# f16 projections in the first attention, and the second attention's maxima, value products, closing steps and roots rearranged

## The reference

```python
# L0 attention: 16 heads of 64, causal
q, k, v = x @ Q_w + Q_b, x @ K_w + K_b, x @ V_w + V_b        # per head
scores = softmax(where(causal, -1e5, q @ k.T / 8))
out = sum_h((scores @ v) @ O_w[h]) + O_b
# L0 feed-forward, 512 wide
h = silu(x @ w1.T * s1) * (x @ w2.T * s2)
h = gelu(h @ h1.T * t1); h = gelu(h @ h2.T * t2); out = h @ w3.T * s3
# L1 attention: 16 heads of 8, not causal, with a Gaussian bias G on the scores
G[q, j] = -2 (j - P[q])**2 / Z[q]**2          # P, Z from tanh and sigmoid of the queries
out = softmax(q @ k.T / sqrt(8) + G) @ v @ wo + bo
# L1 feed-forward
out = x @ (W + up_aux @ lora_up @ lora_down @ down_aux).T + b
```

## Time and profile before

| | |
|---|---|
| median of 3 runs | 1842.44 us (1840.41 to 1842.91) |
| the profiled execution | 1839.43 us, its span 1837.7 us |
| mean granted TensorE clock | 0.962 |
| busy PE, DVE, ACT, POOL | 1607.1, 1268.6, 963.1, 644.1 us |
| first attention | 0 to about 820 us |
| feed-forward and second projections | to about 1053 us |
| second attention | from 1053 us; its turns from 1102 us |

### The profile page before, as it was taken

One profiled execution on the slowest core, in us unless ns is written; L12 is line 12 of the kernel. 1 busy time (PEld: TensorE's weight loads), 2 busy tenths in 40 slices (PEclk: granted clock), 3 DMA queues, 4 the chain that ended last, 5 costly groups with the idle time before them and its releaser, 6 DMA issues. The chain is left out here.

```text
span 1837.7 us, 27256 instructions
## 1 busy us (share of the span) xinstructions
PE 1607.1 (87%) x10432; PEld 497.5 (27%) x10432; DVE 1268.6 (69%) x2301; ACT 963.1 (52%) x1109; POOL 644.1 (35%) x363
## 2 busy tenths in 40 slices
PE   7899999999999999987999468888888888888885
PEld 3233333333333333223444211111111111111122
DVE  5767575766666666613332498888888888888866
ACT  3444444444444444432343306777777777777773
POOL 1587877878788878890000100000000000000000
PEclk8999999999999999997999658999999999999997
DMA  5000000000000000001013420111211211111000
GB/s 133 12 8 12 14 12 13 13 7 13 12 12 14 7 18 7 19 7 32 2 48 71 121 39 9 29 28 29 38 23 23 40 23 23 23 23 23 1 2 23
DMA packets 76212, 46.36 MB, mean 25 GB/s; under 512 B 22159, under 2 KB 74931, under 8 KB 76083
## 3 DMA queue, kind: packets, MB, share of 16 engines
q1 hardware_dynamic: 75266, 44.43, 11.5%
q10 hardware_dynamic: 816, 0.20, 0.0%
HBM read 25.66 MB, written 9.31 MB: 19 GB/s over the span
## 5 line engine op out<-in xcount | busy, mean ns | idle before, releaser
L1465 ACT ACTIVATE probs<-ps_e 128x1024 f32<-128x1024 f32 x512 | 500.1, 1021 | 234.8 <-PE ps_e L1539 233.7
L304 POOL TENSOR_TENSOR acc<-acc,probs 128x1024 f32<-128x1024 f32 (+3 forms) x256 | 502.9, 1964 | 86.5 <-ACT probs L338 65.6
L338 ACT ACTIVATE probs<-ps_e 128x1024 f32<-128x1024 f32 (+1 forms) x320 | 285.7, 901 | 377.5 <-PE ps_e L474 128.6
L1648 DVE TENSOR_REDUCE maxpart<-ps_x 128x2 f32<-128x1024 f32 x351 | 427.8, 1219 | 55.0 <-PE ps_x L1503 52.2
L1549 PE MATMUL ps_o<-probs,v 128*9 128x512 f32 x2048 | 268.7, 597 | 45.4 <-ACT probs L1465 30.0
L491 PE MATMUL ps_o<-probs,v 128*64 128x512 f32 (+3 forms) x1280 | 305.6, 556 | 0.2 <-ACT pv_raw L345 0.2
L582 DVE TENSOR_REDUCE maxpart<-ps_x 128x2 f32<-128x1024 f32 x192 | 234.5, 1221 | 75.7 <-PE ps_x L406 75.7
L1455 POOL TENSOR_TENSOR yt<-x_sb,end_b 128x512 f32<-128x512 f32 x4 | 5.1, 1271 | 749.8 <-DVE x_sb L1709 749.8
L1652 DVE TENSOR_REDUCE maxpart<-ps_y 128x1 f32<-128x512 f32 x322 | 220.2, 684 | 19.0 <-PE ps_y L1503 16.0
L1539 PE MATMUL ps_e<-qrows,krows 62*128 62x512 bf16 x1024 | 221.2, 383 | 6.1 <-DMA qrows<-maxrow 5.5
L1503 PE MATMUL ps_x<-krows,qrows 60*128 60x512 bf16 x702 | 152.7, 402 | 69.4 <-DVE maxpart L1648 68.8
(11 more groups left out here) (247 smaller groups left out, 1460.4 us busy)
## 6 DMA issues: line engine op xcount, KB each, us to landing
qrows<-q_rows SPq DMA_DIRECT2D x64, 192.0 KB
rbc<-rden SPq DMA_DIRECT2D x128, 64.0 KB, 2.1
q_rows<-parts_q SPq DMA_DIRECT2D x24, 128.0 KB, 2.4
k_rows<-parts_k SPq DMA_DIRECT2D x24, 128.0 KB, 2.4
krows<-k_rows SPq DMA_DIRECT2D x16, 192.0 KB, 5.9
raw_h<-in_L_ffn_h_w SPq DMA_DIRECT2D x2, 1024.0 KB, 6.6
w_rows<-parts_w SPq DMA_DIRECT2D x6, 256.0 KB, 2.6
qrows<-a_rows SPq DMA_DIRECT2D x64, 24.0 KB
```

The lines of the kernel that those rows point to most:

```text
L304: pool.tensor_tensor(acc[:, u % 2, :, o:], acc[:, u % 2, :, o:], probs[:, turn % RING, :, o:], ALU.add)\
L338: act.activation(probs[:, turn % RING, :, o:], ps_e[:, turn % 2, :, o:], ACT.Exp, scale=1.0 / math.sqrt(D0))\
L1465: act.activation(probs[:, HG * (turn % 2) + hh], ps_e[:, e % 2], ACT.Exp).then_inc(s_ex, 1)
L1648: dve.reduce_max(maxpart[:, at:at + op[2]], ps_x[:, 0:op[2], :], AX.X).then_inc(s_xf, 1)
```

## The change

In the first attention: the projections of pairs 1 to 7 are three f16 products (high by high, high by low of x, low of the weights by high) in place of one f32 product. The high and low parts of x (written over x_sb) and of the weights (from a staging area in raw["h1"]) are made by POOL ahead of its accumulations. The load of h1 is issued by ACT at turn 8. `out_bias` stands ahead of the eighth maxima block instead of behind turn 1's scores.

In the second attention: ps_x and ps_y become three single banks ps_r, used in turn, each with its own pair of semaphores; every maxima block is a product and a reduction of its own. In a turn the eight blocks go two to a head, "fin" behind the second of them, and "mt" behind all eight. In a unit's second turn the value products are at hh 1 and 3 (`late`). The closing steps have new slots; the first two "ct" stand ahead of the last unit. The roots come from POOL (a power, and for all but the last quarter a Newton round), with statistics and normalization apart on DVE; in the last quarter DVE does one Newton round.

```diff
@@ first attention: loads, splits, projections @@
-            for n, dst in (("k", wk), ("q", wq), ("v", wv)):
-                sp.dma_start(dst[:, 2:, :], a[f"L0_attn_{n.upper()}_w"].rearrange("h m d -> m h d")[:, 2:, :]).then_inc(s_ldw[n], 16)
+            for n in "kq":
+                sp.dma_start(w_stage[n].rearrange("p (h d) -> p h d", d=D0),
+                             a[f"L0_attn_{n.upper()}_w"].rearrange("h m d -> m h d")[:, 2:, :]).then_inc(s_wst, 16)
...
+            for g in range(4):
+                pool.wait_ge(s_xtc[g], 1)
+                if g == 0:
+                    pool.wait_ge(s_xt, 4)
+                pool.tensor_copy(x_part[:, g, 0, :], xt[:, g * QC:(g + 1) * QC]).then_inc(s_hx, 1)
+                pool.wait_ge(s_hx, g + 1)
+                pool.tensor_tensor(x_part[:, g, 1, :], xt[:, g * QC:(g + 1) * QC], x_part[:, g, 0, :], ALU.subtract).then_inc(s_xs, 1)
+            pool.wait_ge(s_wst, 32)
+            for i, n in enumerate("kq"):
...
+                pool.tensor_copy(hi_w, w_stage[n]).then_inc(s_hw, 1)
+                pool.wait_ge(s_hw, i + 1)
+                pool.tensor_tensor(lo_w, w_stage[n], hi_w, ALU.subtract).then_inc(s_ws, 1)
...
+                if turn == 8:
+                    act.wait_ge(s_ws, 2)
+                    act.dma_start(raw["h1"][:, :, :], a["L0_ffn_h1_w"].rearrange("(t p) i -> p t i", p=P)).then_inc(s_ldf, 16)
...
-                w = (wk if n == "k" else wq)[:, 2 * p:2 * p + 2, :].rearrange("m h d -> m (h d)")
-                return pe.matmul(out, w, xt[:, c * QC:(c + 1) * QC], start=True, stop=True)
...
+                for m, (w_at, x_at) in enumerate(((0, 0), (0, 1), (1, 0))):
+                    w = w_part[n][w_at][:, 2 * p - 2:2 * p, :].rearrange("m h d -> m (h d)")
+                    mm = pe.matmul(out, w, x_part[:, c, x_at, :], start=m == 0, stop=m == 2)
+                return mm
...
             for g in range(1, 4):
                 first_values(g)
                 max_products(3 + g)
+            out_bias()
             for b in range(7, EARLY):
                 max_products(b)
...
-                elif turn == 1:
-                    out_bias()
@@ second attention: banks and plan @@
-        ps_x = psum("ps_x1", [P, 2, QC])
-        ps_y = psum("ps_y1", [P, QC])
+        ps_r = psum("ps_r1", [P, 3, QC])
...
+            def place(op, bank=None):
+                k = last.index(min(last)) if bank is None else bank
...
+                bank = 2 if turn >= (NU - 1) * TU - 1 else None
+                if turn < 0:
+                    turns.append([place(op) for op in ops[:BU + 1]] + [place(op) for op in extra] + [place(op) for op in ops[BU + 1:]])
+                else:
+                    turns.append([place(op) for op in ops[:2]] + [place(op, bank) for op in extra if op[0] == "fin"]
+                                 + [place(op) for op in ops[2:]] + [place(op, bank) for op in extra if op[0] == "mt"])
@@ PE's turn loop @@
             for turn, ops in enumerate(TURNS):
-                rest = list(ops)
+                rest, late = list(ops), turn % TU == 1
                 for hh in range(HG):
                     scores(turn, hh)
                     for op in rest[:1]:
                         ring(op)
-                    rest = rest[1:]
-                    if hh % 2 == 0 and turn > 0:
+                    if hh % 2 == late and turn > 0:
                         pv(turn - 1, hh // 2)
-                        if len(rest) > HG - 1 - hh:
-                            ring(rest[0])
-                            rest = rest[1:]
+                    for op in rest[1:2]:
+                        ring(op)
+                    rest = rest[2:]
                     if turn >= (NU - 1) * TU and (turn % TU, hh) in PE_SLOT:
                         step(*PE_SLOT[turn % TU, hh])
                 for op in rest:
                     ring(op)
+                if turn == (NU - 1) * TU - 1:
+                    step("ct", 0)
+                    step("ct", 1)
@@ closing steps and roots @@
+        PE_SLOT = {(0, 1): ("wo", 0), (0, 3): ("wo", 1), (2, 1): ("xt", 0), (2, 3): ("xt", 1), (3, 1): ("ct", 2),
+                   (3, 3): ("ff", 0), (4, 1): ("wo", 2), (4, 3): ("ff", 1), (6, 1): ("xt", 2), (7, 1): ("ff", 2)}
...
+                root = pool.tensor_tensor(rstd[:, m], veps[:, m], power[:, :], ALU.pow)
+                if c < NQ - 1:
+                    chained(root)
+                    chained(pool.tensor_tensor(newton[:, :], rstd[:, m], rstd[:, m], ALU.mult))
+                    chained(pool.tensor_tensor(newton[:, :], newton[:, :], veps[:, m], ALU.mult))
+                    chained(pool.tensor_scalar(newton[:, :], newton[:, :], -0.5, 1.5, ALU.mult, ALU.add))
+                    root = pool.tensor_tensor(rstd[:, m], rstd[:, m], newton[:, :], ALU.mult)
...
-                link(dve.tensor_scalar(t1[:, :].bitcast(I32), veps[:, :].bitcast(I32), 1, None, ALU.arith_shift_right))
-                link(dve.tensor_scalar(rstd[:, :].bitcast(I32), t1[:, :].bitcast(I32), -1.0, float(ROOT_SEED), ALU.mult, ALU.add))
-                for _ in range(3):
...
             def refine(kind, c):
+                link(dve.scalar_tensor_tensor(t1[:, m], veps[:, m], -0.5, rstd[:, m], ALU.mult, ALU.mult))
+                link(dve.tensor_tensor(t1[:, m], t1[:, m], rstd[:, m], ALU.mult))
+                link(dve.scalar_tensor_tensor(rstd[:, m], t1[:, m], 1.5, rstd[:, m], ALU.add, ALU.mult))
```

More of the change, by code:

```diff
@@ L512, in first_values, with out_bias @@
                 values(ps_e[:, g // 2, g % 2], 0, g).then_inc(s_pj, 1)
+            def out_bias():
+                pe.wait_ge(s_ldw["o"], 48)
+                pe.wait_ge(s_xtc[3], 1)
+                for p in range(NPAIR):
+                    mm = pe.matmul(ps_o[:, 0:1], wo[:, p, :], bv[:, p:p + 1], start=p == 0, stop=p == NPAIR - 1)
+                mm.then_inc(s_ob, 1)
             x_features(0)
@@ L538, in _ @@
             pe.wait_ge(s_pjv, 4)
[L539 to L544, removed]
             for turn, (xs, ys) in enumerate(PLAN):
@@ L1396, in build, with blocks_of @@
[L1396 to L1399, removed]
-        X_OPS = sum(op[0] == "x" for ops in PLAN for op in ops)
-        Y_OF["fin", NU - 1] = Y_LAST
-        X_DONE, Y_DONE = {}, {}
-        for ops in PLAN:
-            for op in ops:
-                if op[0] in ("x", "y"):
-                    for b in range(op[1], op[1] + op[2]):
-                        (X_DONE if op[0] == "x" else Y_DONE)[b // BU] = op[3] + 1
+        def blocks_of(turn):
+            if turn < 0:
+                return [("max", b) for b in range(BU + LEAD)]
+            first = BU + LEAD * (turn + 1)
+            return [("max", b) for b in range(first, min(first + LEAD, NU * BU))]
@@ new lines, in plan @@
+        def plan():
+            turns, last, used = [], [-3, -2, -1], [0, 0, 0]
+            def place(op, bank=None):
+                k = last.index(min(last)) if bank is None else bank
+                last[k] = sum(used)
+                used[k] += 1
+                return (*op, k, used[k] - 1)
+            for turn in range(-1, NU * TU):
+                ops, extra = blocks_of(turn), specials(turn)
+                bank = 2 if turn >= (NU - 1) * TU - 1 else None
+                if turn < 0:
+                    turns.append([place(op) for op in ops[:BU + 1]] + [place(op) for op in extra] + [place(op) for op in ops[BU + 1:]])
+                else:
+                    turns.append([place(op) for op in ops[:2]] + [place(op, bank) for op in extra if op[0] == "fin"]
+                                 + [place(op) for op in ops[2:]] + [place(op, bank) for op in extra if op[0] == "mt"])
+            end = place(("fin", NU - 1), 2)
+            steps = {key: place(("step", *key), n % 2)[3:] for n, key in enumerate(STEPS)}
+            return turns, end, steps
@@ L1409, in build @@
+        TURNS, LAST, STEP = plan()
+        BEFORE, TURNS = TURNS[0], TURNS[1:]
+        ALL = [op for ops in [BEFORE] + TURNS for op in ops]
+        RING_AT = {op[:2]: op[2:] for op in ALL + [LAST] if op[0] in ("fin", "mt")}
+        UNIT_END = [{k: max(m for kind, b, kk, m in ALL if kind == "max" and b // BU <= u and kk == k) + 1
+                     for k in range(3)} for u in range(NU)]
         block = ctx.enter_context(nc.Block())
@@ L1452, in _, with chained, refine, residual @@
             pool.tensor_tensor(w_t[:, :], w_t[:, :], w_d[:, :], ALU.add).then_inc(s_wt, 1)
-            for c in range(NQ):
+            steps = [0]
+            def chained(ins):
+                steps[0] += 1
+                ins.then_inc(s_pn, 1)
+                pool.wait_ge(s_pn, steps[0])
+            def refine(kind, c):
+                m = NORM[kind, c] % 2
+                pool.wait_ge(s_sd, NORM[kind, c] + 1)
+                root = pool.tensor_tensor(rstd[:, m], veps[:, m], power[:, :], ALU.pow)
[5 more added lines that the diff above has]
+                    root = pool.tensor_tensor(rstd[:, m], rstd[:, m], newton[:, :], ALU.mult)
```

(3 more changed lines are left out.)

295 lines of the change are left out of this document (154 added, 141 removed).

## The result

The changed kernel takes 1870.48 us (median of 4 runs, 1869.45 to 1871.87) against 1842.07 (4 runs, 1840.41 to 1842.91): a ratio of 1.0156, 95% interval 1.0138 to 1.0173, so 28.4 us slower. I had said 1854 (1826 to 1872). The sign and the range held, the forecast's +12 did not: the loss is more than twice as large. The profiled execution has a span of 1870.2 us and a mean granted clock of 0.941 (before 0.962).

A forecast was written before the change was run, and what follows sets the result against it. PE's issued work was taken to bound the first attention, a loop through PE, DVE and ACT the second. Terms summed to +12.0 on the profiled 1839.43, 1851.4; with the runs' median 3.0 higher, 1854 us, range 1826 to 1872.

The forecast's parts named there:

- first attention: First attention: f16 projections -21, earlier output bias -2.5, moved load of h1 +1, in sum -22.5 us.
- first maxima as singles: Before the second attention's first turn: 72 maxima blocks reduced singly, 3.4 us less, of which -3 was taken.
- units 0 to 13, clock apart: Second attention: late transposition of the maxima makes a unit 46.8 against 44.26 us, +35 in 14 units.
- clock behind the pause: Second attention: PE's pause of about 4 us lowers the clock, 1.3 us in 10 of 14 units, +13.
- unit 14: Second attention: no blocks left in its last turn, transposition early, nothing paid there; -1.6 us.
- last unit and tail: Closing steps' waits and slow spell go, transposes move into the DMA wait, -6.5; two tail roots on POOL, -2.4 us.
- The output bias: First attention's start: moved ahead of a product that waits anyway, about 1 of 3.57 us sticks out; gain 2.5 us.
- The splits on POOL: Start: 13 us of POOL work fits its idle 31.5 us before the first accumulation; free, up to 3 us otherwise.
- The load of h1: First attention: moved to ACT's queue at turn 8, a unit start may wait once for it; +1 us.
- Rival (b): Second attention: PE runs ahead with three banks, turns fall to DVE's 4.85 us, kernel at 1823 us; chance 0.20.
- Rival (a): Second attention: the clock holds through the pause, kernel at 1841 us, no change to be seen; chance 0.18.
- the row of most like size: Tail roots: POOL's power, absent from the trace, priced at 0.45 us like its 128x128 pass; range 0.1 to 1.3.

The follow-up runs named there:

- e4: The changed kernel with the first attention of the kernel before in front of its second one: 1881.42 us, ratio 1.0212 to the kernel before.
- e9: e5's second attention behind the first attention of the kernel before: 1806.2 us, ratio 0.9808 to the kernel before, 9.9 us above e5.
- e2: The changed kernel with 17 unread products added on PE in the pause at the boundary of units 0 to 13: 1849.57 us, ratio 1.004.
- e6: e5 with only the high-part product in the projections of pairs 1 to 7, the two low-part products left out: 1783.7 us, 12.6 less than e5.
- e7: e5 with the sixteen output bias products back behind turn 1's scores, as in the kernel before: 1796.6 us, ratio 0.9757.
- e10: e5 with the addition of the output bias to x done by ACT instead of DVE: 1793.1 us, 3.2 less than e5.
- e1: The changed kernel with the transposition of the maxima behind the fourth of the eight blocks of a unit's last turn: 1825.28 us, ratio 0.9911.
- e5: The changed kernel with the transposition of the maxima behind the second block of a unit's last turn: 1796.3 us, ratio 0.9755.

## Why the prediction was right or wrong

The terms of the forecast beside what the traces and runs showed:

| term | forecast | measured | from |
|---|---|---|---|
| first attention | -22.5 | -10.9 | e4 (e9 gives -9.9) |
| first maxima as singles | -3 | -3.6 | 47.81 to 44.25 us, first block to first score |
| units 0 to 13, clock apart | +35 | +32.2 | e2: first score to 14th interval's end 649.10, before 616.90 |
| clock behind the pause | +13 | +20.9 | e2 |
| unit 14 | -1.6 | -1.5 | e2: 42.05, before 43.54 |
| last unit and tail | -8.9 | -8.3 | last copy to end 66.6, before 74.9 |
| sum | +12.0 | +28.8 | medians: +28.4 |

**The failed step is the first attention**, and in it the sentence that whatever PE is spared "is gained nearly whole". It was off by 11.6 us, of 16.8 in all. Three things in it:

*Size.* A projection saves 0.31, not 0.41. I took the time from start to start of products with 64 rows; the last of the three, followed by a product of another row count, takes 0.31. 56 times 0.31 is 17.4, where the sum had 21. I had named the risk (up to 0.1 more per product) and it came a third of the way.

*What reaches the end.* Only 1.63 us per pair of 8 times 0.31 = 2.48 did (from the ends of the fifth and the 29th unit in the two traces: 9.7 us over six pairs; with the first pair's share some 10.3). This is the largest part of the miss: 7 of the 17.4 us never reached the end. e6 repeats this with another amount: half. PE was busy 79.6 of 80 us, but a product that is issued earlier meets a bank that DVE still holds: PE's waits for DVE grew from 7.7 to 11.0 us between 160 and 700. Over the six pairs, from start to start of PE's instructions, some 4.5 us more pass in front of the three products that wait for DVE (1.2 for the projection, 1.6 for the maxima, 1.8 for the output product), which is most of the 5 us that did not come through there. A full engine in the table by stretches did not mean that its work is the only bound; the ring through DVE was as tight in some turns. Of a pair's eight projections five stand in the unit of 8 turns and one in each other: in the units of 8 turns 1.03 us of 1.55 was gained, in those of 12 turns 0.60 (more than their own 0.31, so some of it seems to come over from the unit before), in those of 4 and 16 turns nothing of the 0.31 each.

*The output bias.* Forecast -2.5, measured 0.3 (e7), which is no change to be seen, since what runs behind it was not followed: DVE's pass of 1.29 us landed beside POOL's accumulation and took 3.40. I had counted the sixteen products and not the DVE pass that hangs on them. e10 shows that it was worth 3.2 us to take it off DVE. The Trainium skill ("SBUF — State Buffer", Who interferes with whom) says of a DVE instruction in a two-port mode, which it says `tensor_scalar` can enter, and one of GpSimd that whichever starts first holds the ports that they share for its whole length, while the other fully blocks. By that rule DVE's pass ends 1.29 after POOL's 39.14, at 40.43; the trace has 40.23, so it agrees within 0.2. That this pass ran in such a mode no row states.

The splits on POOL were hidden, as forecast (done at 26.49). The load of h1, which I had at +1, wasn't tried by itself.

**The clock** was the second miss, 7.9 us. I gave a dip 1.3 us in 10 of 14 units; e2 gives 20.9 in all, 1.5 us for each of 14. The mechanism was right, the share of units too low (some 5 us of the miss) and the price a little low (some 3). The Trainium skill ("TensorE: Matmul & The Clock Gate", Why this matters for your kernels) would have had every unit pay, as I noted; for pauses of about 4 us the runs agree, with half clock behind each of the 14. The gaps that it warns of are longer than e1's of 1.56 to 1.74 us, though, and behind five of those the clock fell as well: here the measurement goes further than the page.

**The unit** came out by its steps. The pause was forecast from the list alone: first value product to first value product over the boundary 9.87, in e2 10.11 (1361.08 to 1371.19); the regular turn 5.17, in e2 5.16 (2.46 + 2.70); the unit without dips 46.8, in e2 46.56; the wait of PE about 4, in the changed kernel 4.17, once per unit. Rival (b), turns at DVE's pace, did not come: the loop closes as walked. Rival (a) is out by e2.

**Last unit and tail** were right in sum and not in their parts. The two tail roots gave 0.42 and 0.48 and not 1.2 each, since the power took 1.02 (inside the bounds of 0.1 and 1.3, but not by "the row of most like size"); the closing steps' waits made up for it. The first power took 1.03 us and the other seven 1.01 to 1.02, so the extra 6 us for a first call from the Trainium skill ("GPSIMD Engine Reference", Instruction dispatch) did not show for this instruction.

## What to carry to other kernels

When an item is moved in a hand-written order, look at what the very next instruction on its engine waits for. The length from the item to its effect (here a copy and a DMA, 3.4 us) has to be covered by work that stands between them in the same queue: behind eight blocks it was covered by nothing (+28 us against the kernel before), behind four by half (-16), behind two almost wholly (-45). The rest of this change gained in sum, and the one place hid it. And do not price a saving on a full engine at its whole length before its neighbours in the loop are seen to have room: here 66% of it reached the end in one case and 51% in the other (e6). Follow every pass that hangs on a moved instruction too.

## What the runs showed of the hardware that I had not expected

- Pauses of PE of 1.56 to 1.74 us in dense work were followed by half clock in five of 14 cases (e1), pauses of 0.2 to 0.6 in none (e5), of 4.0 to 4.2 in all 14 (the changed kernel). In the earlier trace rows 1.65 us had not lowered it, from which I had taken that such a length was safe.
- Seventeen useless products made a kernel 20.9 us faster (e2).
- A power of POOL on 128x4 takes 1.01 to 1.03 us, where a product or a scaling of the same size takes 0.20 and one of 128x128 0.45.
- The last of a run of f16 products of 128 rows takes 0.31 us when a product of 64 rows follows, the others 0.22.
